# Graph attention kernel: adjacency laid out load by load, normalisation on three engines, the own rows' weight blocks on VectorE

## Chip, cores and metric

One Trainium2 chip, one core of it. The metric is the device time of one execution in microseconds. Before the change three runs gave 216.11, 216.38 and 216.88 us, median 216.38.

## The reference

Two graph layers on 4096 nodes with 128 features, each behind a layer norm and a ReLU, each added to its input:

```python
h = jnp.maximum(_layernorm(x, axis=-1), 0.0)
x = x + _L0_gnn_ref(h, adj, L0_gnn_W, L0_gnn_a)
h = jnp.maximum(_layernorm(x, axis=-1), 0.0)
x = x + _L1_gnn_ref(h, adj, L1_gnn_W, L1_gnn_B)
```

The first layer is attention: `Wh = h @ W`, scores `leaky_relu(s[i] + d[j], 0.2)` with `s = Wh @ a[:128]` and `d = Wh @ a[128:]`, kept where `adj[i, j] > 0` or `i == j`, a softmax over j, and the sum of the `Wh[j]` with these weights. The second layer weighs by `exp(-2 (1/adj - 1)^2)` where `adj < 1`, and by zero elsewhere. The adjacency is a 4096x4096 float32 matrix (64 MB) of zeros and ones, about one entry in 2000 set, with low node numbers far more often: the first 128 nodes are hubs. For an entry 0 or 1 the second layer's weight is zero, so the second layer adds nothing.

## The kernel before, in words

The kernel loads the whole adjacency, checks that each entry is 0 or 1 (if any is not, a general path computes everything; it doesn't run here), finds each row's edges and gathers only the nodes that they name. A row's edges are found with TensorE and VectorE: the rows of a 128-row plane are multiplied by powers of two (`pack_w`) and added up in PSUM together with a code of the column (`code_w`, `codes`), so that one word says which of eight rows of a lane have an edge in a column; VectorE takes the largest words (`scan`, `pick`), decodes them into node numbers and bits, POOL gathers the nodes' rows from a table in HBM with indirect DMAs, VectorE weighs them, and TensorE adds them up (`scatter`). Hubs take two other ways: the 128 hub columns of each row (`column`, `add_columns`) and the 128 hub rows (`hub`, `hub_group`) are dense products. The own entry of each row is added by `add_own` with diagonal weight blocks `own_w`.

**Tiling.** The 4096 rows are four supers of 1024. A super has four column groups of 1024, each loaded as two halves: chunk i (0 to 31) is super i // 8, one column group and a half h, 512 rows as 4 planes of 128 x 1024 (2 MB). Super 0 takes the column groups in the order 1, 2, 3, 0, super s starts with group s. Chunks go through a ring of six slots, `adj_ring`.

**Queues.** SP issues the eight loads of x (L391), six chunks, and then a chunk as soon as the slot of the chunk six before is free (L394 to L405): packed by TensorE (`packed`), checked, and for some turned. Stores of finished supers stand behind all loads on the same queue (L386). POOL issues the table's stores (L507) and the gathers (L544); the four groups of eight gathers that may be open wait for `scattered`. Every engine runs its list in order, and the order is written out by hand: for each chunk number, tables such as `WEIGH_AT`, `SCATTER_AT`, `OWN_WEIGHTS_AT` say which other step stands there.

**The prologue** (until about 35 us): for each of eight octants of 512 rows, VectorE computes moments (L1114, L1118), ScalarE the deviation (L912), VectorE inverse and shift (L1124, L1126), ScalarE normalises four blocks (L921), TensorE turns them (L565), ScalarE rectifies (L927), TensorE projects (L577), ScalarE copies (L935). VectorE checks chunks 0 and 1 in the middle of it, and when the projections are there it reduces the ends, makes the tables' factors (until L1556) and goes on to chunk 2. POOL makes `offdiag`, `pack_w` (L466), `codes` and `code_w` first.

**What the change touches.** A check on ScalarE is two passes over a chunk, a sign sum and an absolute sum (L952, L961); one on VectorE is one operation (L1134). `DVE_CHECKED` has 13 chunks, ScalarE the other 19. The diagonal is removed before packing: VectorE multiplies the diagonal blocks by `offdiag` into `clean` for seven chunks (L1158), in place for chunk 6 (L1150), and `pack` then takes these blocks in pieces (L634 to L644). The hub rows lie in the first plane of chunks 0, 2, 4 and 6: TensorE turns them (`turn_hub`, L590), ScalarE copies the result to `hub_mask` (`keep_hub`, L943), VectorE uses it (`hub`, L1419). The hub columns lie in the eight chunks of column group 0: TensorE turns each 128x128 square (`turn_columns`, L609), VectorE multiplies out of PSUM (`column`, L1442). `own_weights` on ScalarE makes eight blocks per super, one activation each (L985).

## Time and profile before

| | |
|---|---|
| median of three runs | 216.38 us (216.11 to 216.88) |
| the profiled execution | 217.44 us, its span 215.6 us |
| granted TensorE clock, mean | 0.909 |
| busy, of the span | PE 72%, DVE 84%, ACT 88%, POOL 62% |
| DMA | 76.81 MB, mean 356 GB/s |
| chain that ended last | DMA 36%, DVE 31%, PE 18%, issue 7%, ACT 5% |

The span runs from the first to the last instruction of the profiled execution; what lies around it (1.8 us here) is the launch. PE is TensorE, PEld its weight loads, DVE VectorE, ACT ScalarE, POOL GpSimd, SP the engine that issues most DMAs. In a table by stretches an engine's busy time stands beside the stretch's length, then the granted clock of TensorE (1.00 is 2.4 GHz), the busy share of the sixteen DMA engines (over 1 where packets overlap) and the rate. A line of instructions gives the engine, the line of the kernel, the operation, what it writes and reads, how many, its busy time and the mean of one, and the idle time before it with what ended it.

### The profile page before, as it was taken

What the parts mean: (1) busy time and instruction counts of PE and PEld (TensorE: products, weight loads), DVE (VectorE), ACT (ScalarE), POOL (GpSimd) and SP (SyncE); (2) the same over time, 40 slices, a digit from 0 to 9 for tenths busy, and PEclk for the clock granted to TensorE, in tenths of its full rate; (3) what the DMA queues carried; (4) which work ended last, traced back from release to release, by engine and by line L of the source; (5) the groups of instructions that cost most, each with busy time, mean ns of one, the idle gap of its engine ahead of it and who ended that gap; (6) DMA issues with size and microseconds to landing.
All of it is one profiled execution on the core that took longest, in us unless ns stands there. A gap on an engine that the chain in (4) does not pass through costs nothing.

```text
span 215.6 us, 3229 instructions
## 1 busy us (share of the span) xinstructions
PE 154.3 (72%) x956; PEld 103.7 (48%) x970; DVE 182.0 (84%) x535; ACT 189.3 (88%) x207; POOL 132.8 (62%) x140
## 2 busy tenths in 40 slices
PE   0186779983794992989929997499392977799472
PEld 0074565440362760549615844186341654668361
DVE  7993999999979999999488796995986499878855
ACT  0699987599899999999999999799999994999960
POOL 3980002295000588888878888888787788667450
PEclk9999999996599698599985999999979799999995
DMA  5999999999999999999999999999999999961303
GB/s 166 355 413 410 410 408 408 409 411 405 418 418 409 409 393 405 391 400 393 402 388 387 394 401 394 404 387 400 394 387 389 386 401 393 406 229 43 115 23 103
DMA packets 22259, 76.81 MB, mean 356 GB/s; under 512 B 2527, under 2 KB 3126, under 8 KB 22240
## 3 DMA queue, kind: packets, MB, share of 16 engines
q1 hardware_dynamic: 18912, 71.31, 84.7%
q0 software_dynamic: 2912, 5.22, 7.0%
q8 instruction: 8, 0.13, 0.2%
q10 hardware_dynamic: 416, 0.07, 0.2%
q14 instruction: 11, 0.09, 0.1%
HBM read 74.06 MB, written 4.23 MB: 363 GB/s over the span
## 4 chain that ended last, share of the span: by engine, by line
DMA 36%; DVE 31%; PE 18%; issue 7%; ACT 5%; SPq 1%; POOL 1%; POOLq 0%; DVEq 0%
DMA adj_ring<-in_adj 35%; DVE summed L1134 10%; PE bank L642 9%; DVE cand L1172 3%; ACT spread L921 3%; DVE hub_w L1415 3%; PE bank L769 2%; DVE x_sb L1458 2%; PE bank L754 2%; PE bank L761 2%; SPq L383 1%; DMA gathered_rows<-node_table,shared_index 1%; DVE stats L1114 1%; PE bank L629 1%; DVE shared_slots L1230 1%
## 5 line engine op out<-in xcount | busy, mean ns | idle before, releaser
L544 POOL DMA_INDIRECT gathered_rows<-node_table,index x48 | 76.0, 1584 | 36.5 <-DVE index L1309 22.5
L952 ACT ACTIVATE trash_a<-adj_ring,below_one 128x4096 fp8e4<-128x4096 f32 x19 | 70.4, 3705 | 5.7 <-DMA adj_ring<-in_adj 5.2
L642 PE MATMUL bank<-adj_ring,pack_w 128*128 128x512 bf16 (+3 forms) x255 | 70.0, 402 | 2.4 <-DMA adj_ring<-in_adj 1.5
L961 ACT ACTIVATE trash_a<-adj_ring 128x4096 fp8e4<-128x4096 f32 x19 | 68.7, 3614 | 0.5
L1134 DVE SCALAR_TENSOR_TENSOR summed<-adj_ring 128x4096 fp8e4<-128x4096 f32 x13 | 58.0, 4458 | 4.3 <-DMA adj_ring<-in_adj 4.2
L642 PEld LDWEIGHTS bank<-adj_ring,pack_w 128*128 128x128 bf16 x262 | 26.1, 104 | 31.5 <-issue 8.8
L544 POOL DMA_INDIRECT gathered_rows<-node_table,shared_index x24 | 33.2, 1382 | 9.6 <-issue 6.7
L1172 DVE MAX8 cand<-bank 128x8 f32<-128x120 f32 (+25 forms) x82 | 23.3, 351 | 3.9 <-PE bank L642 3.9
L769 PE MATMUL bank<-gathered_rows,spread 128*128 128x129 f32 x160 | 20.9, 282 | 3.9 <-DVE spread L1398 2.4
L769 PEld LDWEIGHTS bank<-gathered_rows,spread 128*128 128x128 f32 x160 | 19.4, 194 | 5.1 <-issue 4.8
L629 PE MATMUL bank<-codes,code_w 128*128 128x512 bf16 x25 | 11.2, 448 | 8.5 <-DMA adj_ring<-in_adj 5.6
L678 PE MATMUL bank<-whe,hub_w 128*128 128x129 f32 x64 | 10.4, 316 | 5.1 <-DVE hub_w L1419 5.0
L921 ACT ACTIVATE spread<-x_sb,shift,rstd 128x128 f32<-128x128 f32 x32 | 13.2, 497 | 0.3 <-DVE shift L1126 0.3
L678 PEld LDWEIGHTS bank<-whe,hub_w 128*128 128x128 f32 x64 | 9.1, 219 | 7.0 <-DVE hub_w L1419 6.8
L491 POOL PARTITION_ALL_REDUCE ends_all<-ends x1 | 1.4, 1442 | 17.3 <-DVE ends L1539 17.3
L565 PE MATMUL bank<-ident,spread 128*128 128x128 f32 x32 | 6.3, 327 | 7.8 <-ACT spread L921 7.8
L577 PE MATMUL bank<-w_sb,gathered_rows 128*128 128x130 f32 x64 | 9.8, 300 | 1.4 <-ACT whe L935 1.3
L1442 DVE SCALAR_TENSOR_TENSOR col_w<-r_rows,hub_whe,bank 128x512 f32<-128x512 f32 (+1 forms) x6 | 4.2, 708 | 7.4 <-PE bank L609 7.4
L629 PEld LDWEIGHTS bank<-codes,code_w 128*128 128x128 bf16 x32 | 3.7, 115 | 13.7 <-DMA adj_ring<-in_adj 6.2
L577 PEld LDWEIGHTS bank<-w_sb,gathered_rows 128*128 128x128 f32 x64 | 8.6, 208 | 2.7 <-ACT gathered_rows L927 2.4
L985 ACT ACTIVATE own_w<-ident,w_self 128x128 f32<-128x128 f32 x32 | 9.7, 386 | 0.0
L699 PE MATMUL bank<-slots,own_lane 128*32 128x16 f32 (+1 forms) x24 | 1.4, 188 | 10.5 <-issue 10.5
(190 smaller groups left out, 258.4 us busy)
## 6 DMA issues: line engine op xcount, KB each, us to landing
adj_ring<-in_adj SPq DMA_DIRECT2D x32, 2048.0 KB, 23.6
node_table<-gathered_rows POOLq DMA_DIRECT2D x4, 520.0 KB, 8.3
x_sb<-in_x SPq DMA_DIRECT2D x8, 256.0 KB, 5.9
out<-x_sb SPq DMA_DIRECT2D x3, 512.0 KB, 14.2
gathered_rows<-node_table,index POOLq DMA_INDIRECT x48, 5.9
gathered_rows<-node_table,shared_index POOLq DMA_INDIRECT x24, 5.4
out<-x_sb SPq DMA_DIRECT2D x2, 192.0 KB, 2.1
out<-x_sb SPq DMA_DIRECT2D x1, 128.0 KB, 1.9
```

The costliest lines, as they stand in the source:

```text
L544: pool.indirect_dma_start(out=rows[:, g % RING_GROUPS * GE + t, :], out_offset=None, in_=table, in_offset=bass.IndirectOffsetOnAxis(ap=row ...
L577: last = nc.tensor.matmul(bank[6 + half][:, b * (D + 2):(b + 1) * (D + 2)], hT[:, nb * P:(nb + 1) * P], w0_sb[:, :], start=(b == 0), stop= ...
L629: nc.tensor.matmul(to[:, :], code_w[:, 2 * c + half, :], codes[:, :], start=True, stop=False, skip_group_check=True)
L642: last = nc.tensor.matmul(to[:, lo:hi], pack_w[:, k, :], ring_hi[:, i % AR, row_at + lo:row_at + hi], start=False, stop=(k == KB - 1), ski ...
L678: last = nc.tensor.matmul(bank[7][:, 0:E1], hub_w[:, m % 2, b, :], whe[:, 4 * HUB_ORDER[m] + b, ONE:ONE + E1], start=(m + b == 0), stop=(m ...
L769: return nc.tensor.matmul(acc_of(SUPER_OF_GROUP[g], t), spread[:, g % 2, at * KB:(at + 1) * KB, :], rows[:, g % RING_GROUPS * GE + turn, G ...
L921: last = nc.scalar.activation(hn_block(b), x_sb[:, b, :], ACT.Identity, bias=shift[:, b:b + 1], scale=rstd[:, b:b + 1])
L952: nc.scalar.activation(trash_a[:, :], ring[:, i % AR, :], ACT.Sign, bias=below_one[:, :], scale=-1.0, accum_out=signs[:, n:n + 1], saturat ...
L961: nc.scalar.activation(trash_a[:, :], ring[:, i % AR, :], ACT.Abs, accum_out=sizes[:, n:n + 1], saturate=False).then_inc(checked_a, 1)
L985: last = nc.scalar.activation(own_w[:, t, :], ident[:, :], ACT.Copy, scale=w_self[:, nb:nb + 1])
L1134: nc.vector.scalar_tensor_tensor(trash_v, ring[:, i % AR, :], 1.0, ring[:, i % AR, :], ALU.is_ge, ALU.not_equal, accum_out=bad_v[:, n:n + ...
L1172: last = nc.vector.max(cand[:, at * 8:(at + 1) * 8], word_bank(step, half)[:, lo:hi])
```

## The change

On the host the adjacency is copied into a second input, `adj_laid`, in the order of the loads, with the diagonal set to zero; the own entries become a third, `adj_own`. A load then reads one run of memory; per partition it is cut into two runs (four for the loads 4 to 10). The hub rows become a load of their own behind chunk 2, already turned; the planes that held them are left out of chunks 0, 2, 4 and 6. In the chunks of column group 0 the hub columns' squares lie turned at the end of each partition's row. With that `turn_hub`, `keep_hub`, `turn_columns`, `clean_diagonal` and `clear_diagonal` go, and `hub_mask` is what ScalarE's second pass over the hub load writes. `column` reads the ring, so SP waits for `col_w_set` (VectorE) before it gives such a slot away. VectorE's list of checks loses chunk 1; ScalarE's gains chunk 1 and the hub load and keeps chunk 8. VectorE checks chunk 0 at chunk number 2, behind two row scalings and the first scan. In the prologue POOL normalises two blocks of each octant, ScalarE the other two, VectorE rectifies octants 3 to 7, and POOL makes `pack_w` in between. The own rows' weight blocks are made by VectorE, one product of 128x1024 for a super. `offdiag` and the bit masks are made later.

```diff
-MOMENTS_AHEAD = 3
+MOMENTS_AHEAD = 2
+POOLED = 2
+RECTIFIED_V = [3, 4, 5, 6, 7]
...
+HUB = CHUNKS
+LOADS = [0, 1, 2, HUB] + list(range(3, CHUNKS))
+BESIDE_TABLE = range(4, 11)
+def slot_of(i):
+    return LOADS.index(i) % AR
+def landed(i):
+    return 16 * (LOADS.index(i) // AR + 1)
+def first_plane(i):
+    return 1 if i != HUB and chunk(i)[0] == 0 and chunk(i)[2] == 0 else 0
+def width(i):
+    return CW - P if chunk(i)[1] == 0 else CW
+def runs_of(i):
+    return HK if LOADS.index(i) in BESIDE_TABLE else 2
...
-DVE_CHECKED = [0, 1, 2, 4, 6, 10, 11, 14, 18, 20, 22, 26, 28]
-ACT_CHECKED = [i for i in range(CHUNKS) if i not in DVE_CHECKED]
+DVE_CHECKED = [0, 2, 4, 6, 10, 11, 14, 18, 20, 22, 26, 28]
+ACT_CHECKED = [i for i in LOADS if i not in DVE_CHECKED]
...
-OWN_WEIGHTS_AT = {8: 0, 17: 1, 22: 2, CHUNKS: 3}
+OWN_WEIGHTS_AT = {11: 0, 19: 1, 26: 2, 31: 3}
...
+            def load(i):
+                lo = first_plane(i) * CW
+                laid = adj_laid[LOADS.index(i), 0:P * (HK * CW - lo)]
+                sp.dma_start(ring[:, slot_of(i), lo:HK * CW].rearrange("p (a n) -> p a n", a=runs_of(i)),
+                             laid.rearrange("(a p n) -> p a n", a=runs_of(i), p=P)).then_inc(adj_ready[slot_of(i)], 16)
...
+            for i, old in zip(LOADS[AR:], LOADS):
+                if old != HUB:
+                    sp.wait_ge(packed, old + 1)
+                    if chunk(old)[1] == 0:
+                        sp.wait_ge(col_w_set, 2 * chunk(old)[0] + chunk(old)[2] + 1)
                 if old in DVE_CHECKED:
                     sp.wait_ge(checked_v, DVE_CHECKED.index(old) + 1)
                 else:
                     sp.wait_ge(checked_a, ACT_CHECKED.index(old) + 1)
-                load_chunk(i)
+                load(i)
...
+            def normalise(o):
+                pool.wait_ge(shift_set, o + 1)
+                pool.wait_ge(rstd_set, o + 1)
+                if o >= 4:
+                    pool.wait_ge(hT_done, o - 3)
+                for b in range((o + 1) * BPO - POOLED, (o + 1) * BPO):
+                    last = nc.gpsimd.tensor_scalar(hn_block(b), x_sb[:, b, :], rstd[:, b:b + 1], shift[:, b:b + 1],
+                                                   ALU.mult, ALU.add)
+                last.then_inc(hn_done_pool, 1)
...
+            for o in range(XO):
+                normalise(o)
+                nc.gpsimd.tensor_scalar(pack_w[:, o, :], ident[:, :], EDGE * 2 ** o, None, ALU.mult).then_inc(code_set, 1)
...
+                act.dma_start(own_adj[:, :], adj_own).then_inc(own_loaded, 16)
...
-                nc.scalar.activation(trash_a[:, :], ring[:, i % AR, :], ACT.Abs,
+                nc.scalar.activation(hub_mask_row if i == HUB else trash_a[:, :], ring[:, slot_of(i), :], ACT.Abs,
                                      accum_out=sizes[:, n:n + 1], saturate=False).then_inc(checked_a, 1)
...
-                if i in OWN_WEIGHTS_AT:
-                    own_weights(OWN_WEIGHTS_AT[i])
-                if i == CHUNKS - 1:
-                    own_weights(SG - 1)
+                if LOADS[LOADS.index(i) - 1] == HUB:
+                    check(HUB)
                 if i in ACT_CHECKED:
                     check(i)
-                if chunk(i)[0] == 0 and i % 2 == 0:
-                    keep_hub(i)
...
+            def rectify(n):
+                dve.wait_ge(hT_done, n + 1)
+                nc.vector.tensor_scalar(hT[:, n * 512:(n + 1) * 512], bank[4 + n % 2][:, :], 0.0, None,
+                                        ALU.max).then_inc(hT_copied_v, 1)
...
+            def own_weights(s):
+                dve.wait_ge(self_set, 1)
+                if s:
+                    dve.wait_ge(own_added, s)
+                blocks = slice(s * KB, (s + 1) * KB)
+                nc.vector.tensor_tensor(own_w[:, :, :],
+                                        ident[:, :].rearrange("p (o n) -> p o n", o=1).broadcast_to([P, KB, P]),
+                                        w_self[:, blocks].rearrange("p (t o) -> p t o", o=1).broadcast_to([P, KB, P]),
+                                        ALU.mult).then_inc(own_w_set, 1)
...
-            for i in range(2):
-                check(i)
-
...
             for i in range(2, CHUNKS):
-                if i in CLEANED and i < 2 * CC + 2:
-                    clean_diagonal(i)
-                if i in DVE_CHECKED and i not in CHECK_LATE.values():
-                    check(i)
                 if i == 2:
                     scale_rows(1)
                     scale_rows(2)
+                    scan(0)
+                    check(0)
+                if i in DVE_CHECKED and i not in CHECK_LATE.values():
+                    check(i)
```

## Rows read from the trace of the kernel before

**Rows 1.** Busy time by stretches: length, five engines, clock, DMA share, GB/s.
```profile
17.00:42.00 25.00, 19.84 (x125) 13.26 (x125) 21.22 (x41) 20.60 (x54) 1.80 (x2) 1.00 1.03 409
...
70.00:170.00 100.00, 77.49 (x463) 50.58 (x471) 82.98 (x217) 97.56 (x74) 81.80 (x55) 0.88 1.03 395
170.00:192.50 22.50, 18.07 (x133) 13.08 (x135) 21.06 (x51) 18.80 (x13) 17.51 (x11) 1.00 0.98 379
192.50:215.60 23.10, 14.00 (x109) 11.48 (x108) 15.79 (x69) 15.91 (x20) 10.73 (x10) 0.89 0.23 71
```

**Rows 2.** The page's DMA issues: size of one, median us from issue to landing.
```profile
adj_ring<-in_adj SPq DMA_DIRECT2D x32, 2048.0 KB, 23.6
```

**Rows 3.** The last load's issue (start, length), its landing, and the packing behind it.
```profile
171.18 1.61 SPq L383 DMA_DIRECT2D adj_ring<-in_adj  x1
...
adj_ring<-in_adj SPq DMA_DIRECT2D x1, 2048.0 KB, 21.3
...
192.57 1.98 PE L642 MATMUL bank<-adj_ring,pack_w 128*128 128x512 bf16 x8
```

**Rows 4.** DMA packets from 7.0 to 8.6 us, then from 17 to 42 us.
```profile
DMA packets 327, 0.60 MB, mean 375 GB/s; under 512 B 34, under 2 KB 34, under 8 KB 327
...
q1 hardware_dynamic: 327, 0.60, 102.4%
...
q1 hardware_dynamic: 2567, 10.19, 102.1%
```

**Rows 5.** Groups of instructions, the whole span: busy us, mean ns, idle before.
```profile
L952 ACT ACTIVATE trash_a<-adj_ring,below_one 128x4096 fp8e4<-128x4096 f32 x19 | 70.4, 3705 | 5.7 <-DMA adj_ring<-in_adj 5.2
L921 ACT ACTIVATE spread<-x_sb,shift,rstd 128x128 f32<-128x128 f32 x32 | 13.2, 497 | 0.3 <-DVE shift L1126 0.3
L577 PE MATMUL bank<-w_sb,gathered_rows 128*128 128x130 f32 x64 | 9.8, 300 | 1.4 <-ACT whe L935 1.3
L985 ACT ACTIVATE own_w<-ident,w_self 128x128 f32<-128x128 f32 x32 | 9.7, 386 | 0.0
L1359 DVE TENSOR_TENSOR spread<-edge_w,lane_of_p 128x1024 f32<-128x1024 f32 x6 | 7.4, 1225 | 0.2
L565 PE MATMUL bank<-ident,spread 128*128 128x128 f32 x32 | 6.3, 327 | 7.8 <-ACT spread L921 7.8
L1158 DVE TENSOR_TENSOR clean<-adj_ring,offdiag 128x512 bf16<-128x512 f32 x7 | 4.8, 683 | 0.7 <-DMA adj_ring<-in_adj 0.7
L466 POOL TENSOR_SCALAR pack_w<-ident 128x128 bf16<-128x128 f32 x8 | 4.1, 533 | 0.3
```

**Rows 6.** Waits of VectorE: us in total, times, longest.
```profile
DVE col_w L1442 <- PE bank L609: 7.4, 2, 4.3
```

**Rows 7.** Two gathers of POOL and a check of VectorE: start, length.
```profile
179.68 1.00 POOL L544 DMA_INDIRECT gathered_rows<-node_table,shared_index  x1 [0.30 <-issue]
180.98 5.01 POOL L544 DMA_INDIRECT gathered_rows<-node_table,shared_index  x1 [0.30 <-issue]
...
180.70 4.42 DVE L1134 SCALAR_TENSOR_TENSOR summed<-adj_ring 128x4096 fp8e4<-128x4096 f32 x1
```

**Rows 8.** The prologue's steps in order of time, and the sixth load's landing.
```profile
9.36 1.65 ACT L921 ACTIVATE spread<-x_sb,shift,rstd 128x128 f32<-128x128 f32 x4 [0.35 <-DVE shift L1126]
...
18.48 18.34 SPq L383 DMA_DIRECT2D adj_ring<-in_adj  x2
...
31.18 0.83 ACT L935 ACTIVATE whe<-bank 128x260 f32<-128x260 f32 x2 [0.42 <-PE bank L577]
...
34.56 0.68 DVE L1556 TENSOR_TENSOR spread<-whe,bits_i 128x512 f32<-128x512 f32 x1
...
39.51 2.37 DVE L1142 TENSOR_TENSOR gathered_rows<-whe 128x1032 f32<-128x1032 f32 x2
...
41.79 1.61 DVE L1172 MAX8 cand<-bank 128x8 f32<-128x120 f32 x7
...
adj_ring<-in_adj SPq DMA_DIRECT2D x1, 2048.0 KB, 24.0
```

More of the change, by code:

```diff
@@ L122 @@
 CHECK_LATE = {22: 22, 27: 26, 29: 28}
-SCAN_AT = {2 * n + 2: n for n in range(STEPS - 1)}
+SCAN_AT = {2 * n + 2: n for n in range(1, STEPS - 1)}
 PICK_AT = {8: 0, 16: 1, 24: 2, 30: 3}
@@ L391, in _ @@
                 sp.dma_start(x_sb[:, o * BPO:(o + 1) * BPO, :], x_octants[o // 2, o % 2]).then_inc(x_loaded[o], 16)
-            for i in range(AR):
-                load_chunk(i)
-            for i in range(AR, CHUNKS):
-                old = i - AR
-                sp.wait_ge(packed, old + 1)
-                if chunk(old)[1] == 0:
-                    sp.wait_ge(col_turned, 2 * chunk(old)[0] + chunk(old)[2] + 1)
-                if chunk(old)[0] == 0 and chunk(old)[2] == 0:
-                    sp.wait_ge(hub_turned, old + 2)
+            for i in LOADS[:AR]:
+                load(i)
[4 more added lines that the diff above has]
+                        sp.wait_ge(col_w_set, 2 * chunk(old)[0] + chunk(old)[2] + 1)
                 if old in DVE_CHECKED:
@@ L518, in _ @@
                 store_rows(s)
+            for k in range(KB):
+                nc.gpsimd.memset(bit_mask[:, k:k + 1], 1 << (12 + k)).then_inc(tail_set, 1)
+                nc.gpsimd.memset(shared_mask[:, k:k + 1], 1 << (14 + k)).then_inc(tail_set, 1)
+                nc.gpsimd.memset(oct_mask[:, k:k + 1], 1 << (15 + k)).then_inc(tail_set, 1)
+            nc.gpsimd.memset(full[:, :, :], 0.0).then_inc(tail_set, 1)
+            nc.gpsimd.tensor_scalar(offdiag[:, :], ident[:, :], -1.0, 1.0, ALU.mult, ALU.add).then_inc(offdiag_set, 1)
             pool.wait_ge(hub_whe_loaded, 16)
@@ L631, in pack @@
                     for k in ks:
[L632 to L644 removed]
+                        w = width(i) - BW if half == 0 else BW
+                        at = first * CW + (k % HK - first) * width(i) + half * (width(i) - BW)
+                        last = nc.tensor.matmul(to[:, BW - w:BW], pack_w[:, k, :], ring_hi[:, slot_of(i), at:at + w],
+                                                start=False, stop=(k == KB - 1), skip_group_check=True)
                 last.then_inc(packed, 1)
@@ L993, in _ @@
                     deviations(o + MOMENTS_AHEAD)
-                if o >= 1:
+                if o >= 1 and o - 1 not in RECTIFIED_V:
                     rectify(o - 1)
@@ L1409, in hub @@
                     dve.wait_ge(a_set, 1)
-                dve.wait_ge(hub_kept, 2 * (next(i for i in range(0, 2 * CC, 2) if chunk(i)[1] == n // 2) // 2) + n % 2 + 1)
+                if m == 0:
+                    dve.wait_ge(checked_a, ACT_CHECKED.index(HUB) + 1)
                 if m >= 2:
@@ L1696, with laid_out @@
 _INS = ["x", "adj", "L0_gnn_W", "L0_gnn_a", "L1_gnn_W", "L1_gnn_B"]
+def laid_out(arrays, np):
+    adj = arrays["in_adj"]
+    apart = adj.copy()
+    np.fill_diagonal(apart, 0)
+    laid = np.zeros((len(LOADS), P * HK * CW), adj.dtype)
+    for n, i in enumerate(LOADS):
+        if i == HUB:
+            block = apart[:P].reshape(P, CC, P, KB).transpose(2, 1, 3, 0)
+        else:
+            s, c, h = chunk(i)
+            rows = slice(s * HR + h * HK * P, s * HR + (h + 1) * HK * P)
+            block = apart[rows, c * CW:(c + 1) * CW].reshape(HK, P, CW).transpose(1, 0, 2)[:, first_plane(i):]
+            if c == 0:
+                squares = block[:, :, 0:P].reshape(LANES, KB, -1, P).transpose(3, 1, 2, 0)
+                block = np.concatenate([block[:, :, P:].reshape(P, -1), squares.reshape(P, -1)], axis=1)
+        block = block.reshape(P, runs_of(i), -1).transpose(1, 0, 2).reshape(-1)
+        laid[n, 0:block.size] = block
+    return {"adj_laid": laid, "adj_own": np.ascontiguousarray(np.diagonal(adj)).reshape(P, NB)}
 def kernel(**inputs):
```

248 lines of the change are left out of this document (86 added, 162 removed).

## The prediction, made before the change was run

> **What bounds the kernel now.** I read the table by stretches first, because every engine is busy for most of the span and the page's shares don't say which of them the others wait for. From 17 to 192.5 us the sixteen DMA engines are taken at 0.98 to 1.03 in every stretch, at 409 GB/s while only the adjacency moves and at 395 and 379 GB/s beside the gathers; behind 192.5 us the share is 0.23 [rows 1]. So up to 192.5 us the span is as long as the bytes take. It is not a lack of free slots: a load takes 23.6 us in the median from issue to landing, against some 5 us that its own 2 MB need, so about four loads always stand in line [rows 2].
>
> Then the hand-over at the end. The last load is issued at 171.18 and takes 21.3 us, so it lands at 192.5, and TensorE starts packing it at 192.57 [rows 3]. From there to the end of the span at 215.6 us, 23.1 us, runs the tail: scan, pick, decode, gather, scatter, last store. So the sum has three terms: the start up to the first packet, the stream, the tail. The profiled execution took 217.44 us for its span of 215.6; the three runs' median is 216.38, 1.06 us under it, and I move the median by what the span moves.
>
> **Bytes.** The hub's 128 rows become a load of their own (2 MB) and leave four loads of super 0 (0.5 MB each), the rest is only reordered: 64 MB before, 64 MB after, in 33 loads where there were 32. The own entries (16 KB) come through ScalarE's queue beside x: under 0.1 us at 409 GB/s. SP issues one load more, at a time when it waits for room in the queue anyway. Nothing here shortens the stream by bytes.
>
> **Packets.** Before, a load is 512 runs of 4 KB. After, 24 loads of 2 MB are laid out as 256 runs of 8 KB and two loads of 1.5 MB as 256 of 6 KB; seven keep four runs per partition. The trace has two sizes: 2 KB runs (x) go at 375 GB/s with the engines full, 4 KB runs at 409 [rows 4]. A load of 2.10 MB takes 5.13 us at 409 and 5.59 at 375: 0.46 us for twice the packets, so half the packets should give back 0.23 us, 24 x 0.23 = 5.6 us. That is the one end. The other comes from the packets' own time: 1.024 x 1.6 us x 16 / 327 = 80 ns against 1.021 x 25 us x 16 / 2567 = 159 ns; twice 80 is 0.8% more than 159, half of that on 24 loads of 5.13 us is 0.5 us. The first end rests on 1.6 us in which the first loads are only starting, so it is too large; the second misses gaps between packets, because the packets overlap (shares over 1), so it is too small. I take 2.5 us, nearer to the second, which stands on packets alone, and keep 0.5 and 5.6 for the range. The Trainium skill (DMA: Bandwidth & Descriptors, sections "Measured" and "iDMA fabric") has 425 GB/s for one 16 MB transfer and 408.7 for a stream with 4 KiB rows; if the gap is cost per packet, 8 KB would run at 417, and 50.3 MB at that rate instead of 409 would save 2.4 us (an estimate from that page).
>
> **Work taken off the engines.** All of this lies beside the stream and I count it as zero:
> - ScalarE loses 32 own-weight blocks (9.7 us), half of the 32 normalisations (6.6 of 13.2 us) [rows 5] and the hub mask's evictions, and gains two checks, chunk 1 and the hub, of two passes of 3.7 us and some 0.4 us of reads (2 x 7.8 = 15.6 us). Chunk 8 is ScalarE's before and after. Net about even.
> - VectorE loses chunk 1's check (4.4), a quarter of four checks (4 x 1.1), seven clean-ups and one in place (8 x 0.68 = 5.4) and the waits for the turned columns (7.4 idle) [rows 5 to 7]. It gains four own-weight products of 128x1024 (4 x 1.22 = 4.9, from the spread of that size) and five rectifications (about 0.6 each, an estimate from the 128x512 product of 0.68). Some 6 us fewer, and the idle time.
> - TensorE loses 63 turning matmuls and the cut-up matmuls around the diagonal.
>
> The cover is the line of four loads. If the stream were not there, these would be worth several us; as it is, they let each chunk be consumed nearer to its landing. What that is worth in the tail is small: packing the last chunk began 0.05 us behind its landing [rows 3]. It matters only so that the tail can follow if the stream ends earlier: the engines have to be 2.5 us earlier too, and the 7.4 us that VectorE no longer idles, 4.3 of them in one piece, covers that.
>
> **What the own weights now hold up.** The four products are queued on VectorE ahead of the next scan or weigh. Behind the last one stand weighing group 7 and the last scan. What stands ahead of it on VectorE comes earlier, since the column weights no longer wait, so I count zero, at most its own 1.2. They also meet POOL: a gather took 1.00 us, and the next one, beside a check of 4.4 us on VectorE, 5.01 [rows 7]. So a product beside a gather costs POOL between nothing and its own 1.2 us, at most 4.9 in all; VectorE drops more work than that from POOL's stretch (clean-ups and quarters of checks, 9.8 us), and I count zero again. The Trainium skill (SBUF — State Buffer, "Who interferes with whom") lets a VectorE operation with two SBUF inputs hold up a GpSimd operation that reads SBUF; the products are of that kind, and the gather above agrees with such a hold.
>
> **The start of the stream.** Here is the wait that the change adds. The first six loads are now 10.5 MB, not 12, and the seventh needs chunk 0's check, which moves from the idle middle of the prologue to behind two row scalings and the first scan. The sixth load was issued at 18.48 and landed 24.0 us later, at 42.5; 1.5 MB less is 3.8 us less, so the line is empty at 38.7 [rows 8]. The prologue: the last projection is copied at 32.0 now. ScalarE's part shrinks by 6.6 us and by five rectifications; then TensorE's 6.3 + 9.8 = 16.1 us, begun at 9.4, is the next limit, at 25.5; POOL's two blocks and one weight block per octant (3 x 0.53 x 8 = 12.7) fit beneath it [rows 5, 8]. So 6.5 us earlier. VectorE's last product of this stage ended at 35.2, then 28.7. On top: two scalings 2.4, scan 1.6, three quarters of a check 3.3: the seventh load is issued at 36.0, 2.7 us ahead of the empty line [rows 8]. Zero, with little to spare.
>
> **Sum.** 216.38 - 2.5 = 213.9 (profiled: 217.44 - 2.5 = 214.9, span 213.1).
>
> **Rivals.**
> A. The packets save nothing: long runs are cut up again, or the memory sets the rate. For: the 0.5 us end; against: 375 to 409 GB/s from one doubling. Time 216.4, or 215.9 with the 0.5. The Trainium skill (DMA: Bandwidth & Descriptors, "Where 436 GB/s comes from") says that the memory's share of about 358 GB/s binds such loads, which would make packet size irrelevant; the trace's 409 GB/s is above it.
> B. Slower: the line runs empty. If POOL's normalisation costs more than its 0.53 us, or VectorE's in-order rectifications make the engines wait for each other, the prologue keeps its old length: chunk 0's check then ends at 35.2 + 7.3 = 42.5, 1 us later the first packet, 43.5 against 38.7: 4.8 us without data. The time is 216.4 + 4.8 - 2.5 = 218.7. It decides from a check that ends behind 37.7, and outweighs the saving from 40.2 on. For: a margin of only 2.7 us, on estimates; against: 9.6 us of ScalarE's prologue go elsewhere.
> C. Gathers wait behind packets of twice the length: they land later, VectorE weighs later, and slots come free late. Even so the line of four loads covers it until the tail, where no load is left. Under 1 us, 215.
>
> **How the numbers follow.** Forecast 213.9 at 0.64 with its own range 210.8 (5.6 saved) to 215.7; A 0.16 at 215.8 to 216.4; B 0.15; C 0.05, half of it still faster. Two runs of this kernel can be told apart from 0.65 us on (0.3%). Faster: 0.64 and half of C, 0.67. Same: A, 0.16. Slower: B and what is left, 0.17. The range goes from 210.8 to 217.6; it leaves out most of B and the larger savings, under 0.2 together.
>
> **What would show it.** Right: the DMA share stays at 1 from 17 us on, the rate without gathers rises from 409 towards 417, the mean load-to-load distance falls by 0.1 us, the last load lands near 190, and the tail behind it stays 23 us. The prologue's last copy stands near 25.5 and the seventh load is issued by 36. Wrong: a gap in the DMA row between 35 and 45 us (B); 409 GB/s as before (A); or a tail whose length has changed, which no step of mine gives.

## The result, and the profile after

The changed kernel takes 218.72 us in the median of four executions (218.54 to 219.84), the one before 216.27 beside it: ratio 1.0119, 95% interval 1.0079 to 1.0158. It is slower by 1.2%, and the interval doesn't reach 1; the forecast was 213.9. The ratios of the experiments leave out executions that lie over 1.5% above the fastest of their kernel, so where many do, the median of all stands beside the ratio.

The table by stretches of the changed kernel, columns as in [rows 1]:

```profile
17.00:42.00 25.00, 20.14 (x113) 12.17 (x112) 19.33 (x50) 20.75 (x35) 8.11 (x19) 1.00 0.85 332
42.00:70.00 28.00, 13.78 (x40) 5.37 (x42) 21.88 (x55) 27.66 (x19) 9.33 (x33) 0.70 1.02 407
70.00:170.00 100.00, 76.03 (x427) 48.82 (x434) 86.43 (x216) 92.26 (x56) 79.50 (x52) 0.88 1.02 406
170.00:192.50 22.50, 17.03 (x124) 12.24 (x126) 18.11 (x48) 19.85 (x13) 18.16 (x14) 1.00 1.01 404
192.50:216.80 24.30, 15.49 (x115) 13.09 (x113) 17.15 (x71) 14.15 (x12) 11.51 (x11) 0.86 0.26 81
```

Two things changed in opposite directions. Beside the gathers the stream is quicker, 406 and 404 GB/s where it was 395 and 379 [rows 1]. From 17 to 42 us the DMA share is 0.85 where it was 1.03. The page's DMA rows (40 slices of 5.4 us) show where:

```profile
DMA  5999996699999999999999999999999999971312
GB/s 158 353 429 416 419 403 263 193 404 371 421 417 418 422 406 417 401 413 400 410 404 399 399 411 405 408 408 403 411 399 400 407 408 400 415 275 41 115 23 103
```

Slices seven and eight, 32.5 to 43.4 us, hold 263 and 193 GB/s. What happened stands in the timeline of these microseconds, VectorE with POOL, then the load queue and TensorE:

```profile
26.70 0.56 DVE L1518 TENSOR_REDUCE ends<-whe 128x1 f32<-128x32 f32 x4 [1.88 <-ACT whe L930]
30.31 0.38 POOL L518 PARTITION_ALL_REDUCE ends_all<-ends  x1 [6.52 <-issue]
30.73 0.15 DVE L1531 TENSOR_SCALAR neg_dmax<-ends_all 128x1 f32<-128x1 f32 x1 [2.14 <-POOL ends_all L518]
31.55 2.38 DVE L1121 TENSOR_TENSOR gathered_rows<-whe 128x1032 f32<-128x1032 f32 x2
33.84 1.61 DVE L1151 MAX8 cand<-bank 128x8 f32<-128x120 f32 x7
35.37 3.35 DVE L1113 SCALAR_TENSOR_TENSOR summed<-adj_ring 128x3072 fp8e4<-128x3072 f32 x1
38.81 19.60 SPq L407 DMA_DIRECT2D adj_ring<-adj_laid  x6
46.74 1.46 PE L639 MATMUL bank<-adj_ring,pack_w 128*128 128x512 bf16 x3 [6.03 <-DMA adj_ring<-adj_laid]
```

And the DMA issues of two stretches, the seventh load and the last, with the time from issue to landing at the end of the line:

```profile
adj_ring<-adj_laid SPq DMA_DIRECT2D x1, 2048.0 KB, 7.9
...
adj_ring<-adj_laid SPq DMA_DIRECT2D x1, 2048.0 KB, 20.2
```

The seventh load is issued at 38.81, right behind the check of chunk 0, and lands 7.9 us later, at 46.70. The sixth had landed at 37.98: the DMA engines ran dry. The rate from 34 to 47 us, in 40 slices of 0.325 us, shows both edges of the hole:

```profile
GB/s 397 425 378 397 356 217 142 95 76 47 19 0 0 0 0 0 0 13 176 25 101 290 227 403 403 403 416 416 429 416 441 429 416 403 429 403 400 419 425 416
```

It falls from 35.6 us on, over two microseconds before the sixth load has landed; the first bytes of the seventh come about 1 us behind its issue, and the full rate only from 41.5. Counted in bytes: at 46.70 the changed kernel has 12.5 MB of the adjacency. The one before had 12 MB at 42.46 [rows 8] and the next 2 MB at 47.58, so 12.5 MB at 43.74. The lines for that, the seventh load of the kernel before and its time to landing:

```profile
36.46 4.44 SPq L383 DMA_DIRECT2D adj_ring<-in_adj  x3
...
adj_ring<-in_adj SPq DMA_DIRECT2D x1, 2048.0 KB, 11.1
```

At this point the changed kernel is 2.96 us behind. From there to the last landing the kernel before needs 148.78 us, the changed one 192.85 - 46.70 = 146.15: 2.63 us less, the longer runs' part. The last load (issued at 172.69, 20.2 us) lands 0.33 us later than before [rows 3]. The tail behind it is 24.0 us, where it was 23.1. The chain of work that ended last (start, length, what) now comes out of the gathers:

```profile
181.63 5.01 POOL gathered_rows L577
186.63 0.30 issue
186.94 6.37 DMA gathered_rows<-node_table,shared_index
193.38 0.44 DVE same L1327
193.85 0.43 DVE same L1330
194.31 1.24 DVE spread L1344
195.54 0.14 issue
195.68 2.04 PE bank L767 x16
```

A gather beside VectorE's check of chunk 28 took 5.01 us, and the last gather of group 7 landed at 193.3, 0.5 us behind the last load; VectorE's weighing waited for it. Further on TensorE's clock stood at 0.55 between 202.9 and 206.4, and adding the own rows took 3.57 us instead of 2.05. How much of the 0.9 us each of them makes isn't shown.

2.96 - 2.63 + 0.9 is the 1.2 us by which the spans differ (215.6 and 216.8). The medians differ by 2.45: the profiled execution of the kernel before lay 1.17 us over its median, that of the changed one on it; what makes executions of one kernel differ by that much isn't shown.

### The profile page after: what moved, and what is told of

Its sections match the earlier page's. It is cut to its first block, busy times and chain, and to the rows that moved or that the text cites. A ratio compares the mean times of both kernels' runs of the same rounds, so it can differ in the third digit from the quotient of the medians.

```text
span 216.8 us, 2976 instructions
## 1 busy us (share of the span) xinstructions
PE 150.6 (69%) x853; PEld 99.1 (46%) x865; DVE 177.7 (82%) x536; ACT 184.5 (85%) x155; POOL 139.6 (64%) x155
## 3 DMA queue, kind: packets, MB, share of 16 engines
q1 hardware_dynamic: 12784, 71.31, 82.4%
## 4 chain that ended last, share of the span: by engine, by line
ACT 28%; DMA 25%; POOL 13%; PE 12%; issue 11%; DVE 10%; POOLq 0%; DVEq 0%; ACTq 0%; SPq 0%
DMA adj_ring<-adj_laid 20%; ACT trash_a L939 14%; ACT trash_a L948 10%; POOL gathered_rows L577 9%; DMA gathered_rows<-node_table,shared_index 4%; PE bank L639 3%; PE bank L617 3%; PE bank L767 2%; ACT hub_mask L948 2%; PE bank L605 1%; DVE x_sb L1434 1%; DVE shared_slots L1209 1%; DVE gathered_rows L1104 1%; PE bank L759 1%; PE bank L752 1%
## 5 line engine op out<-in xcount | busy, mean ns | idle before, releaser
L939 ACT ACTIVATE trash_a<-adj_ring,below_one 128x4096 fp8e4<-128x4096 f32 x21 | 77.8, 3706 | 7.3 <-DMA adj_ring<-adj_laid 6.4
L639 PE MATMUL bank<-adj_ring,pack_w 128*128 128x512 bf16 (+1 forms) x239 | 69.7, 423 | 13.8 <-DMA adj_ring<-adj_laid 12.8
L948 ACT ACTIVATE trash_a<-adj_ring 128x4096 fp8e4<-128x4096 f32 x20 | 72.3, 3614 | 0.5
L1113 DVE SCALAR_TENSOR_TENSOR summed<-adj_ring 128x4096 fp8e4<-128x4096 f32 (+1 forms) x12 | 50.3, 4189 | 6.5 <-issue 3.4
L577 POOL DMA_INDIRECT gathered_rows<-node_table,shared_index x24 | 28.9, 1203 | 9.8 <-issue 7.0
L1151 DVE MAX8 cand<-bank 128x8 f32<-128x120 f32 (+25 forms) x82 | 23.4, 352 | 7.0 <-PE bank L639 7.0
L759 PE MATMUL bank<-whe,own_w 128*128 128x129 f32 x64 | 9.4, 310 | 0.0
L759 PEld LDWEIGHTS bank<-whe,own_w 128*128 128x128 f32 x64 | 8.9, 222 | 0.2
L1395 DVE TENSOR_SCALAR hub_w<-r_hub,whe 128x128 f32<-128x128 f32 x32 | 8.8, 350 | 0.0
L491 POOL TENSOR_SCALAR spread<-x_sb,rstd,shift 128x128 f32<-128x128 f32 x16 | 7.2, 456 | 2.4 <-DVE shift L1099 2.2
L930 ACT ACTIVATE whe<-bank 128x260 f32<-128x260 f32 x16 | 6.1, 387 | 3.0 <-PE bank L617 2.4
```

The source lines that it names most:

```text
L577: pool.indirect_dma_start(out=rows[:, g % RING_GROUPS * GE + t, :], out_offset=None, in_=table, in_offset=bass.IndirectOffsetOnAxis(ap=row ...
L639: last = nc.tensor.matmul(to[:, BW - w:BW], pack_w[:, k, :], ring_hi[:, slot_of(i), at:at + w], start=False, stop=(k == KB - 1), skip_grou ...
L759: last = nc.tensor.matmul(acc_of(s, t), own_w[:, t, :], whe[:, s * KB + t, ONE:ONE + E1], start=False, stop=True, skip_group_check=True)
L939: nc.scalar.activation(trash_a[:, :], ring[:, slot_of(i), :], ACT.Sign, bias=below_one[:, :], scale=-1.0, accum_out=signs[:, n:n + 1], sat ...
L948: nc.scalar.activation(hub_mask_row if i == HUB else trash_a[:, :], ring[:, slot_of(i), :], ACT.Abs, accum_out=sizes[:, n:n + 1], saturate ...
L1113: nc.vector.scalar_tensor_tensor(trash_v[:, first_plane(i) * CW:HK * CW], data, 1.0, data, ALU.is_ge, ALU.not_equal, accum_out=bad_v[:, n: ...
```

## The experiments

"Landed" is the last load's issue and its time to landing, added up; "31 packed" is when TensorE begins to pack the last chunk. These and the span come from the one profiled execution of each kernel, which can lie off the median of all its executions (2.7 us over it for "all together", 1.6 under it for "packs first").

| kernel | landed | 31 packed | span | ratio to before (95%) |
|---|---|---|---|---|
| before | 192.5 | 192.57 | 215.6 | 1 |
| changed | 192.9 | 193.06 | 216.8 | 1.0119 (1.0079 to 1.0158) |
| early check | 189.0 | 190.92 | 213.8 | 0.9912 (0.9880 to 0.9944) |
| POOL sooner | 191.4 | 193.15 | 216.7 | 1.0074 (1.0040 to 1.0109) |
| 4 KB runs | 195.4 | 195.45 | 218.0 | 1.0160 (1.0118 to 1.0201) |
| before, 8 KB runs | 188.8 | 188.87 | 213.8 | 0.9899 (0.9849 to 0.9948) |
| early check, chunk 28 on ScalarE | 188.6 | 190.65 | 214.3 | 0.9886 (0.9827 to 0.9945) |
| early check, own weights on ScalarE | 188.5 | 191.73 | 215.3 | 0.9985 (0.9948 to 1.0023) |
| early check, 16 KB runs | 186.9 | 192.13 | 215.1 | 0.9955 (0.9911 to 0.9998) |
| early check, 4 KB runs | 193.0 | 193.01 | 216.2 | 1.0071 (1.0042 to 1.0100) |
| early check, chunk 28 on ScalarE, packs first | 188.5 | 192.93 | 216.0 | 1.0160 (1.0117 to 1.0202) |
| early check, filled tail | 189.8 | 189.85 | 213.3 | 0.9922 (0.9892 to 0.9951) |
| before again | not in the trace | 192.56 | 215.4 | 0.9999 (0.9977 to 1.0021) |
| all together | 189.8 | 191.66 | 215.1 | 0.9863 (0.9807 to 0.9918) |
| before, late check | 196.6 | 196.61 | 220.0 | 1.0249 (1.0191 to 1.0308) |

**The dry stretch.** First the check of chunk 0 is taken away from behind scalings and scan:

```diff
             rectify(7)
+            check(0)
             dve.wait_ge(whe_copied, 2 * XO)
...
                     scan(0)
-                    check(0)
```

> The changed kernel with VectorE's check of chunk 0 taken out from behind the row scalings and the first scan and put into the prologue, ahead of its wait for the projections. T1 (the stream runs dry because the seventh load waits for that check): the check ends near 28, the seventh load is issued near 31 to 32, when chunk 0 is packed, instead of 38.8; the DMA row shows no dip between 32 and 43 us; the 2.96 us are won back and the time is 218.7 - 3.0 = 215.7. T3 (the tail is 0.9 us longer because the gathers are late against the last load, whatever the start does): the tail behind the last landing stays near 23.9 us. If the late landing alone had made the tail longer, it goes back to 23.1 and the time is 214.9. Rival (the dip isn't the cause, engines further on set the time): no change, 218.7.

The check ended at 28, the seventh load was issued at 33.26 (its issue, and its time to landing), and the page's DMA row shows no dip:

```profile
33.26 6.42 SPq L407 DMA_DIRECT2D adj_ring<-adj_laid  x2
...
adj_ring<-adj_laid SPq DMA_DIRECT2D x1, 2048.0 KB, 9.8
```

```profile
DMA  5999999999999999999999999999999999941312
```

The seventh load landed at 43.07, 3.6 us sooner than in the changed kernel: that is the cost of the dry stretch by itself, and the 2.96 above are what was left of it after the longer runs had saved 0.7 us in the first six loads. The last load landed 3.8 us sooner and the span fell by 3.1 us; the tail stayed long (24.7 us). The ratio went from 1.012 to 0.991 (over all twelve executions the median is 216.15, where the kernel before had 216.75 beside it). The step was then put into the kernel before, alone:

```diff
-DVE_CHECKED = [0, 1, 2, 4, 6, 10, 11, 14, 18, 20, 22, 26, 28]
+DVE_CHECKED = [1, 0, 2, 4, 6, 10, 11, 14, 18, 20, 22, 26, 28]
...
-SCAN_AT = {2 * n + 2: n for n in range(STEPS - 1)}
+SCAN_AT = {2 * n + 2: n for n in range(1, STEPS - 1)}
...
-            for i in range(2):
-                check(i)
+            check(1)
...
+                if i == 2:
+                    scale_rows(1)
+                    scale_rows(2)
+                    scan(0)
+                    check(0)
                 if i in DVE_CHECKED and i not in CHECK_LATE.values():
                     check(i)
-                if i == 2:
-                    scale_rows(1)
-                    scale_rows(2)
```

> The kernel before, with VectorE's check of chunk 0 alone moved behind the two row scalings and the first scan, as in the change; chunk 1's check stays in the prologue, layout and loads as before. The first six loads hold 12 MB and land by 42.4. VectorE's prologue still ends at 35.2, scalings and scan take 4.0, the check 4.4: it ends at 43.6, the seventh load is issued at 43.7 and its first packets follow some 2 us later. T1: the stream stands for some 3 us, the DMA row dips near 42 to 46 us, the last load lands near 195.5 and the time is 216.4 + 3.0 = 219.4. Rival (a late seventh load is made good by the loads behind it, and the changed kernel lost its time elsewhere): 216.4 to 217.

In its timeline stand the check and the issue of the seventh load, and below that the page's DMA row:

```profile
39.53 4.40 DVE L1134 SCALAR_TENSOR_TENSOR summed<-adj_ring 128x4096 fp8e4<-128x4096 f32 x1
...
44.04 0.92 SPq L383 DMA_DIRECT2D adj_ring<-in_adj  x2
```

```profile
DMA  5999999289999999999999999999999999982302
```

The check ended at 43.9, the seventh load was issued at 44.04 and landed 7.5 us later; the stream came 4.1 us late to its end and the kernel was 2.5% slower. Each way, this one step moves the time by more than the changed kernel lost. So the dry stretch by itself is enough, and it is the cause.

**Why the check was so late.** It was forecast for 36.0. Of the 2.8 us, 1.2 were the last copy (26.67, not 25.5). Another 1.7 lies between that and VectorE's last product, 3.2 us before and 4.9 after: VectorE waits for POOL's all-reduce. The next kernel brings POOL to it sooner:

```diff
+            pool.wait_ge(small_set, 4)
+            for b in range(N // BW):
+                nc.gpsimd.memset(code_w[64:128, b, :], float(BW * b // 64)).then_inc(code_set, 1)
+            pool.wait_ge(code_set, N // BW)
+            nc.gpsimd.memset(whe[:, :, ONE], 1.0).then_inc(one_set, 1)
+            pool.wait_ge(one_set, 1)
             pool.wait_ge(ident_set, 1)
...
             for o in range(XO):
                 normalise(o)
-                nc.gpsimd.tensor_scalar(pack_w[:, o, :], ident[:, :], EDGE * 2 ** o, None, ALU.mult).then_inc(code_set, 1)
+                for k in {XO - 2: (o, o + 1), XO - 1: ()}.get(o, (o,)):
+                    nc.gpsimd.tensor_scalar(pack_w[:, k, :], ident[:, :], EDGE * 2 ** k, None,
+                                            ALU.mult).then_inc(code_set, 1)
```

> The changed kernel with POOL's nine memsets of code_w and whe moved ahead of its normalisations and the last pack_w block ahead of the last two, so that POOL comes to the all-reduce of the ends some 2 us earlier (21.5 instead of 23.8). First theory (the all-reduce needs some 6.5 us from the moment at which POOL comes to it, hidden before the change, where POOL stood there from 15.7 on): the all-reduce stands near 28.0 instead of 30.3, VectorE goes on 2 us sooner, check of chunk 0 ends near 36.5, the dip shrinks to under 1 us and the time is 216.5 to 217. Rival (the all-reduce is late for the ends, or for VectorE's products beside it, which end at 28.6): it stays near 30.3 and the time stays 218.7.

POOL's timeline in that kernel, then in the early-check kernel:

```profile
28.33 0.78 POOL L522 PARTITION_ALL_REDUCE ends_all<-ends  x1 [6.49 <-DVE ends L1522]
37.01 0.41 POOL L525 TENSOR_SCALAR bad<-end_max 128x1 f32<-128x1 f32 x1 [7.89 <-issue]
```

```profile
30.07 0.39 POOL L518 PARTITION_ALL_REDUCE ends_all<-ends  x1 [6.30 <-issue]
38.68 1.38 POOL L521 TENSOR_SCALAR bad<-end_max 128x1 f32<-128x1 f32 x1 [8.22 <-issue]
```

In three kernels the all-reduce stands 6.3 to 6.5 us behind POOL's work before it, whenever the ends are ready (27.3, 27.5 and 28.5), and here, where POOL came to it 1.9 us sooner than in the changed kernel, it stood 2.0 us sooner. In the kernel before POOL had been there since 15.7 and, by this reading, paid the 6.4 us while it waited. The Trainium skill (GPSIMD Engine Reference, "2.1 Instruction dispatch") gives about 6 us for the first call of a freshly loaded kernel of POOL's own code; the three waits are near that. That code is loaded in them no trace shows. The seventh load was issued at 37.41, the last landed 1.4 us sooner, and the ratio is lower by 0.45%, about 1.0 us, with intervals that overlap. That is less than forecast; the tail was longer (25.3 us).

**The longer runs.**

```diff
 def runs_of(i):
-    return HK if LOADS.index(i) in BESIDE_TABLE else 2
+    return HK
```

> The changed kernel with four runs per partition in every load (4 KB, in the short loads 3 to 4 KB) in place of two: packets as before the change, all else changed. T2 (8 KB runs are worth 2.6 us of the stream): 218.7 + 2.6 = 221.3, with the stream at 409 GB/s where no gathers run. Rival (the loads are quicker because each now reads one stretch of memory, not because of longer runs): 218.7, no change.

The last load lands 2.55 us later, the time grows by 0.4% (0.9 us, and the intervals overlap): the tail is shorter here, 22.6 us. The loads still read one stretch of memory each, so the rival is out. The same size with the early check, and the layout alone in the kernel before:

> The version with the early check of chunk 0, with four runs per partition in all loads: everything of the change but the longer runs, and without the dry stream. By the prediction's terms the rest of the change is worth nothing, since the line of loads covers it: the last load lands near 192.0 (before the change 192.5) and the time is that of the kernel before, 216.0 to 216.8. Rival (the work taken off the engines shortens the tail or the stream by itself): under 215.5.

> The kernel before, with only the layout in memory changed: each chunk lies in one stretch and a partition's share is cut into two runs of 8 KB (four of 4 KB for loads 4 to 10), no hub load, nothing moved between engines, twelve MB in the first six loads. T2: the stream is 2.4 to 2.6 us shorter and the tail the same, so 216.3 - 2.5 = 213.8. Rival (the engines' work before the change couldn't follow an earlier stream, so the rest of the change is needed): 215.5 to 216.3.

```diff
-                sp.dma_start(ring[:, i % AR, :].rearrange("p (k n) -> p k n", k=HK),
-                             adj_chunks[s, c, h]).then_inc(adj_ready[i % AR], 16)
+                sp.dma_start(ring[:, i % AR, :].rearrange("p (a n) -> p a n", a=runs_of(i)),
+                             adj_laid[i].rearrange("(a p n) -> p a n", a=runs_of(i), p=P)).then_inc(adj_ready[i % AR], 16)
```

With a full stream 8 KB runs bring the last landing forward by 3.9 us (189.0 against 193.0) and by 3.7 (188.8 against 192.5), more than the 2.5 forecast. Of the ratio it is 1.6% (3.4 us) with the rest of the change and 1.0% (2.2 us) without it. The early check with 4 KB is no equal of the kernel before: 0.7% slower, 1.5 us, of which its trace shows 0.5 in the stream; so the rest of the change isn't worth zero but a little less, and where is open. And the layout alone, in the kernel before, comes to 0.990, as low as the whole change with the dry stretch repaired (0.991): the kernel before could follow the earlier stream, so the rival there is out, and no gain of the rest of the change can be seen. Twice the length again:

> The version with the early check of chunk 0, with one run of 16 KB per partition (12 KB in the short loads) where it had two, four still in loads 4 to 10. If a packet's fixed cost is what the longer runs save (0.1 us for a load of 256 packets fewer): 128 packets fewer in 24 loads are another 1.2 us, the last load lands near 187.8 instead of 189.0, and the time is up to 1.2 us less. Rival (runs over 8 KB are cut up again, or the engines wait for each other): packets of 8 KB as before and no change.

The last load lands another 2.1 us sooner, with a quarter fewer packets on the load queue (9456 for 12784 in the changed kernel), so the runs are not cut up again. But the time is no lower: 0.996 against 0.991 with overlapping intervals, and over all twelve executions of each a median of 217.67 against 216.15. The page's DMA issues (median us from issue to landing at the end) show a longer way of the gathers, with 4 KB, 8 KB and 16 KB runs, each with the early check:

```profile
gathered_rows<-node_table,index POOLq DMA_INDIRECT x48, 5.5
```

```profile
gathered_rows<-node_table,index POOLq DMA_INDIRECT x48, 5.9
```

```profile
gathered_rows<-node_table,index POOLq DMA_INDIRECT x48, 6.6
```

Whether these 0.7 us set the time isn't shown: chunk 31 was also packed 5.2 us behind its landing, of which more below.

**The tail.** In the early-check kernel chunk 31 is packed 1.9 us behind its landing. Three kernels ask why.

```diff
-DVE_CHECKED = [0, 2, 4, 6, 10, 11, 14, 18, 20, 22, 26, 28]
+DVE_CHECKED = [0, 2, 4, 6, 10, 11, 14, 18, 20, 22, 26]
...
-NAL = 3
+NAL = 4
-CHECK_LATE = {22: 22, 27: 26, 29: 28}
+CHECK_LATE = {22: 22, 27: 26}
```

> The version with the early check of chunk 0, and chunk 28's check moved from VectorE to the end of ScalarE's list (22 checks instead of 21). T3 (a gather beside that check takes 5.0 us instead of 1.0, and the last gather of group 7 then sets when the tail can go on): group 7's last gather starts 3 to 4 us sooner than 183.4, so the scatter of group 7 no longer waits and follows the packing of the last chunk; the tail behind the last landing falls from 24.7 to some 23.5 us: 1 us faster than the version with the early check. Rival (the tail's length comes from TensorE's clock, whatever the gathers do): the tail stays at 24.5 or more, with the clock near 0.76 in its second half, no change. ScalarE's last check should end near 211, in time for the flag; if not, up to 1 us slower.

The last gather of group 7 started at 179.3 instead of 183.4, as said, but chunk 31 was still packed 2.1 us late, the tail was 25.7 us and the ratio is no different. So in this version that gather doesn't set the end.

```diff
-ADD_COLUMNS_AT = {13: 0, 21: 1, 28: 2}
-ADD_OWN_AT = {13: 0, 21: 1, 29: 2}
+ADD_COLUMNS_AT = {13: 0, 21: 1, 30: 2}
+ADD_OWN_AT = {13: 0, 21: 1, 30: 2}
```

> The version with the early check of chunk 0 and chunk 28's check on ScalarE; TensorE adds super 2's hub columns and own rows behind the packing of chunk 30 instead of chunks 28 and 29. Theory (once the last load lands before 190 us, TensorE's own list sets the end: it stood from 174.7 to 178.0 for VectorE's epilogue of super 1 ahead of packing chunk 29, and so packed chunk 31 from 190.65 on, 2.1 us behind its landing): chunk 29 is packed as it lands, near 178 instead of 181.3, chunk 31 is packed within 0.5 us of its landing, and the time is 1.5 to 2 us less than that version, 213 to 213.5. Rival (the gathers of the last super, or VectorE's own list, hold the end): chunk 31 is packed sooner but the scan and scatter behind it aren't; no change.

A miss: 1.6% slower than the kernel before. TensorE packed chunk 29 at its landing, then stood 2.69 us for the picks, and the two moved steps came ahead of chunk 31 (packed at 192.93).

```diff
             add_columns(SG - 1)
+            pe.wait_ge(scanned, 2 * STEPS)
+            for _ in range(9):
+                nc.tensor.matmul(bank[3][:, :], code_w[:, 0, :], codes[:, :], start=True, stop=True, skip_group_check=True)
             place_shared(4)
```

> The version with the early check of chunk 0, and nine matmuls of 128x512 (some 1.9 us, into a bank that nobody reads again) where TensorE stands idle in the tail, between the last super's hub columns and the shared words (197.2 to 199.6). Theory (part of the longer tail is TensorE's clock: it fell to 0.50 from 199.6 to 203 behind that idle stretch, and adding the own rows took 3.48 us instead of 2.05): the clock stays at 1.00 there, the own rows take 2.05 and the time is up to 1.4 us less. Rival (the clock falls by what came earlier, or the next step waits for VectorE anyway): no change, or the fall only comes later.

By stretches, early check first, then filled:

```profile
196.00:199.60 3.60, 1.27 (x12) 1.08 (x10) 3.33 (x18) 3.57 (x4) 2.92 (x3) 1.00 0.50 177
199.60:203.00 3.40, 3.30 (x15) 3.28 (x16) 2.72 (x14) 3.37 (x3) 1.13 (x3) 0.53 0.15 33
```

```profile
196.00:199.60 3.60, 3.11 (x18) 1.76 (x18) 2.92 (x20) 3.59 (x2) 0.99 (x1) 1.00 0.51 175
199.60:203.00 3.40, 2.20 (x20) 2.04 (x19) 2.48 (x9) 3.38 (x2) 2.23 (x2) 1.00 0.03 9
```

With TensorE busy for 3.11 of 3.60 us the clock stayed at 2.4 GHz and the own rows took 2.05 us; with 1.27 it fell to 1.2 GHz and they took 3.48. The idle stretch alone doesn't decide: of thirteen profiled executions without the fillers seven fell there (own rows 3.20 to 3.81 us) and six did not, the kernel before among these. Of two with them none fell, which is few beside six of thirteen. The ratio is the same as with the early check alone, so the time shows no clear gain. In this execution chunk 31 was packed at its landing, 189.85. That was ahead of the fillers and isn't their doing. From 180 to 184 us, early check first, then filled:

```profile
180.00:184.00 4.00, 4.00 (x18) 2.24 (x17) 2.70 (x4) 3.97 (x4) 3.69 (x2) 0.66 1.01 402
```

```profile
180.00:184.00 4.00, 3.51 (x24) 2.50 (x22) 2.56 (x11) 3.97 (x4) 3.37 (x4) 1.00 1.02 424
```

The same holds in all fourteen executions whose last landing is in the trace. In seven the clock stood at 1.2 GHz for a time within the last 10 us before that landing (early check, POOL sooner, chunk 28 on ScalarE, own weights on ScalarE, 16 KB runs, packs first, all together), and these packed chunk 31 1.7 to 5.2 us late; in the other seven it did not, and they packed it within 0.2 us. So the lateness goes with TensorE's clock and not with the place of a check. TensorE at full clock can follow the earlier stream (before, 8 KB runs: 188.82 and 188.87); why the clock falls in one and not in the next was not found, and no run here forces it.

**The own rows' weight blocks.** The title's part, undone on the early check (eight activations per super on ScalarE, the product on VectorE gone):

```diff
-OWN_WEIGHTS_AT = {11: 0, 19: 1, 26: 2, 31: 3}
+OWN_WEIGHTS_AT = {8: 0, 17: 1, 22: 2, CHUNKS: 3}
```

> The version with the early check of chunk 0, with the own rows' weight blocks made by ScalarE again, eight activations for a super, at the chunk numbers of the kernel before. T4 (the prediction's zero: both engines' work lies beside the stream): within 0.5 us of the version with the early check. First rival (VectorE's products hold up gathers and the last weighing, at most 1.2 us in the tail): up to 1.2 us faster. Second rival (ScalarE, with 21 checks of 7.7 us each, is what feeds the stream, so 9.7 us more on it delay the loads): slower by 1 to 5 us, with a dip in the DMA row.

By the ratios 0.7% slower than with VectorE's products (1.6 us), but over all twelve executions of each the medians are 216.84 and 216.15, and each kernel's own executions spread over 3 to 5 us. So the two counts give 1.6 and 0.7 us, and a gain of the title's part isn't shown. The stream has no dip and ends no later, so the second rival is out. Chunk 31 was packed 3.2 us late, and the clock had fallen ahead of it here too.

**Two last ones.**

> The kernel before, unchanged, profiled once more beside these. The profile on which the prediction rested was 1.1 us over the median of its kernel. If the stream's length is the same in every execution, the last load lands at 192.5 again and the difference lies in the tail; if not, it lies in the stream.

The last landing isn't in this trace, but chunk 31 is packed at 192.56, where the first profile had 192.57, and the span ends 22.9 us later. This profiled execution too lay over its median (217.24 and 216.62). The profile doesn't show where the others are shorter.

> The changed kernel with all that helped or did no harm: check of chunk 0 early, POOL's memsets ahead of the normalisations, chunk 28's check on ScalarE, and the nine filling matmuls in the tail. If the gains were independent: 1.0 from POOL, up to 0.5 from chunk 28 and a steady clock on top of 214.9, so 213.5, and the last load lands near 188.5. Rival (with the last load landing before 190, TensorE's list and the last super's gathers hold the end, so that nothing at the start counts any more): 214.5 to 215, as with the early check alone, with chunk 31 packed 1.5 to 2 us behind its landing.

The lowest ratio of all, 1.4% under the kernel before, but within the intervals no different from the early check with chunk 28 on ScalarE. The ratio comes to some 213.4 us, which is what the sum of the gains gave, and not the rival's 214.5 to 215. But none of the gains is clear of its own interval, and the last load landed at 189.8, not at 188.5, so this agreement may be luck. Chunk 31 was packed 1.9 us behind its landing as the rival had it, in a profiled execution of 216.94 us, 2.7 over the median, and with the clock down ahead of it; what the quicker executions did isn't in the trace.

## Why the prediction was wrong

- **Bound, bytes.** Right but for the start: from 52 us to the last landing the DMA engines are full in every kernel here, and 64 MB in 33 loads flowed as said.
- **Packets.** The mechanism was right and rival A is out. 2.5 us were forecast; 2.63 in the changed kernel (counted from 46.7 us on), 3.7 and 3.9 over a whole stream without a hole, inside the bounds of 0.5 and 5.6. From 18 to 31 us the kernel before moves 416 GB/s with 8 KB runs and 408 with 4 KB. The estimate of 417 from the Trainium skill (DMA: Bandwidth & Descriptors, "Measured" and "iDMA fabric") agrees with that.
- **The start of the stream.** The step that failed: zero, "with little to spare", measured 2.96 us against the kernel before, and 3.6 against the same kernel without the hole. The margin of 2.7 us (issue at 36.0, line empty at 38.7) became a lack of 0.8 (38.81 and 37.98), and the hole was longer than that. Four terms were off. First, the copies ended 1.2 us later: TensorE, set down for 25.5, ended at 26.24, and the last copy, which the sum leaves out, 0.43 us behind it. Second, the ends-to-product stretch was carried over at 3.2 us and was 4.9, because it had hidden the all-reduce's 6.4 us behind a POOL that had been idle for 17 us; I moved work onto POOL and did not ask what its idle time had paid for. Third, the line was empty 0.7 us sooner: 38.7 counts 1.5 MB less, but not that the longer runs bring these loads in faster (in the kernel before, they alone bring the sixth landing from 42.46 to 41.9). Fourth, a load's issue was compared with the moment at which the line is empty. A load into an empty line takes 7.5 to 7.9 us from issue to landing where its 2 MB need 5.1, 2.4 to 2.8 us more; rival B allowed 1 us for it, the zero nothing. With the line empty at 38.0, the load had by that to be issued at about 35.4, an estimate: loads issued at 33.9 or sooner left no hole, one at 37.4 did. The forecast 36.0 was late for that; against its own 38.7 it would have been just in time. Rival B's empty line came true, with the gap in the DMA row that was named as its sign, but not its reason: the prologue did get shorter (last copy at 26.67 for 32.0), and POOL's normalisations took 0.46 us each, under the 0.53. Its 218.7 is the measured number by luck, with a gap of 2.96 instead of 4.8 and the rest from the tail and from where the profiled execution lay.
- **Engines' work, own weights: zero.** Lost in the stream for the changed kernel, as said. With the stream repaired the own weights on VectorE give 1.6 or 0.7 us by the count, which the spread of the executions doesn't bear out as a gain, and the engines' work as a whole nothing or a little less than nothing (0.7% with 4 KB runs).
- **The tail stays 23 us.** Wrong for most: 24.0 in the changed kernel, 24.7 with the early check, 25.0 with the layout alone, 28.2 with 16 KB, but 23.4 with the filled tail. "The engines have to be 2.5 us earlier too" was the right condition; VectorE's idle time doesn't cover it, for TensorE packed late in every execution in which its clock had fallen shortly ahead of the last landing.
- **Rival C.** Its first step is seen: a gather takes 5.5 us in the median beside 4 KB runs, 5.9 beside 8 KB and 6.6 beside 16 KB. The 5.9 on the page of the kernel before counts only the 24 of 48 gathers whose landing is in its trace; the three kernels with 4 KB runs that have all 48 show 5.5 to 5.6. What it costs in time isn't shown.

Repaired by the one move, the changed kernel comes to 0.991 of the kernel before, about 214.9, or to 216.15 against 216.75 if every execution counts: the forecast's direction, one to two microseconds short of it, and no more than the longer runs give alone.

## What to carry over

When a check that frees a buffer is moved, find the moment at which the queue behind it runs empty and subtract what a load into an empty queue takes beyond its bytes (2.4 to 2.8 us here); the check has to end before that. A saving that empties the queue sooner shortens this margin too. An engine that waits long ahead of an operation may be paying its start-up there, so give that wait a price before filling it. And a saving in a full stream only counts as far as the engines behind it can end sooner: here 3.7 and 3.9 us of landing gave 2.2 and 3.4 us of time by the ratios.

## What was not expected of the hardware

- POOL's all-reduce stood 6.3 to 6.5 us behind the instruction before it wherever POOL came to it late, and the next ordinary operation came 7.2 us (before), 7.9, 8.0 and 8.2 us behind the all-reduce. No run here tells what the second is.
- Runs of 16 KB moved the last load 2.1 us forward against 8 KB and raised the gathers' median from 5.9 to 6.6 us.
- The same kernel step takes 2.05 us or up to 3.81 by TensorE's clock, and the clock falls in one version and not in the next at the same place. Where it had fallen shortly before the last landing, the last chunk was packed 1.7 to 5.2 us late; where it hadn't, within 0.2 us.
